# Four output products of a batch in the loop of the values' turn, output weights rounded a step later, in the first attention of a two-layer decoder kernel

## The reference

```python
def _L0_attn_ref(x, Wq, Wk, Wv, Wo):          # NH = 16, hd = 32
    q = (x @ Wq.T).reshape(B, T, NH, hd).transpose(0, 2, 1, 3)   # k and v alike
    att = einsum('bhtd,bhsd->bhts', q, k) / sqrt(hd) + causal mask
    w = softmax(att, axis=-1)
    z = einsum('bhts,bhsd->bhtd', w, v).transpose(0, 2, 1, 3).reshape(B, T, D)
    return z @ Wo.T
x = x + _L0_attn_ref(_layernorm(x), Wq, Wk, Wv, Wo)
```

## Time and profile before

| | us |
|---|---|
| median of 3 runs | 1908.64 (1906.13 to 1909.9) |
| the profiled execution | 1907.17 |
| its span, first to last instruction | 1905.7 |
| PE busy in the span | 1805.5 |
| DVE, ACT, POOL busy | 1113.3, 807.4, 1010.0 |
| mean granted PE clock | 0.986 |

### The profile page before, as it was taken

The page is one execution under the profiler, slowest core; times in us unless marked ns, Lnnn a source line. Parts: engine busy times, 40 slices in busy tenths (PEclk is TensorE's granted clock), DMA queues, the critical chain, the costliest instruction groups (busy, mean ns, idle before and its releaser), DMA issues. The chain is left out here.

```text
span 1905.7 us, 30804 instructions
## 1 busy us (share of the span) xinstructions
PE 1805.5 (95%) x10161; PEld 1565.8 (82%) x10167; DVE 1113.3 (58%) x2769; ACT 807.4 (42%) x2063; POOL 1010.0 (53%) x965
## 2 busy tenths in 40 slices
PE   7999989999999999999888999999999999999996
PEld 5888858788999999899667888888888888867795
DVE  6676785763333333335766666666666757566345
ACT  3767633222222222221256566666665433543231
POOL 3444341397883957895457456456453203116783
PEclk9999999999999999999999999999999999999998
DMA  3556430236653645554343234233331210012666
GB/s 116 173 155 205 144 138 0 78 145 226 231 199 126 214 144 180 191 153 127 90 112 95 68 92 117 57 89 93 84 78 56 74 50 1 24 50 84 213 214 195
DMA packets 104551, 232.54 MB, mean 122 GB/s; under 512 B 20672, under 2 KB 20928, under 8 KB 101328
## 3 DMA queue, kind: packets, MB, share of 16 engines
q1 hardware_dynamic: 84080, 144.31, 25.0%
q0 software_dynamic: 19744, 85.47, 13.6%
q10 hardware_dynamic: 576, 0.79, 0.2%
HBM read 126.23 MB, written 57.93 MB: 97 GB/s over the span
## 5 line engine op out<-in xcount | busy, mean ns | idle before, releaser
L712 POOL TENSOR_SCALAR a_E<-a_E,a_inv 128x128 f32<-128x128 f32 (+3 forms) x384 | 213.9, 575 | 237.7 <-DVE a_inv L848 237.7
L745 ACT ACTIVATE a_E<-a_E,a_top 128x512 f32<-128x512 f32 (+3 forms) x384 | 211.1, 565 | 6.0 <-DVE a_top L842 5.9
L153 PE MATMUL bank<-f_UH,f_XH 128*128 x596 | 200.5, 336 | 8.4 <-POOL f_UL L165 3.4
L153 PE MATMUL bank<-f_UL,f_XH 128*128 x596 | 193.2, 324 | 0.0
L153 PE MATMUL bank<-f_UH,f_XL 128*128 x596 | 193.2, 324 | 0.0
L842 DVE CUSTOM_DVE_ANT_0 a_E<-a_causal,bank 128x512 f32<-128x512 bf16 (+3 forms) x384 | 163.6, 480 | 43.0 <-PE bank L1023 31.5
L153 PE MATMUL bank<-a_PHL,a_VH 128*128 128x512 f32 (+3 forms) x768 | 181.1, 325 | 0.9 <-issue 0.6
L737 ACT ACTIVATE a_PHL<-bank 128x512 fp32r<-128x512 f32 (+1 forms) x288 | 131.0, 528 | 112.6 <-PE bank L1039 112.5
L1821 ACT ACTIVATE f_HH<-bank 128x256 fp32r<-128x256 f32 x220 | 59.8, 323 | 232.2 <-PE bank L2218 232.1
L165 DVE TENSOR_TENSOR a_PHL<-bank,a_PHL 128x512 fp32r<-128x512 f32 (+1 forms) x288 | 153.2, 585 | 5.1 <-ACT a_PHL L737 4.8
L1876 DVE TENSOR_TENSOR f_gate<-bank,f_gate 128x352 f32<-128x352 f32 x79 | 41.3, 522 | 192.1 <-PE bank L153 192.0
(11 more groups left out here) (407 smaller groups left out, 4864.8 us busy)
## 6 DMA issues: line engine op xcount, KB each, us to landing
f_uraw<-f_up POOLq DMA_DIRECT2D x18, 1408.0 KB, 6.7
f_xb<-table SPq DMA_DIRECT2D x86, 256.0 KB, 3.2
table<-f_ob SPq DMA_DIRECT2D x86, 256.0 KB, 2.7
table<-a_zeros SPq DMA_DIRECT2D x31, 512.0 KB, 4.3
f_draw<-f_down POOLq DMA_DIRECT2D x27, 512.0 KB, 4.5
a_g<-a_f SPq DMA_DIRECT2D x160, 64.0 KB, 2.0
a_raw<-a_qkv SPq DMA_DIRECT2D x36, 256.0 KB
f_uraw<-f_up POOLq DMA_DIRECT2D x9, 704.0 KB, 4.4
```

The lines of the kernel that those rows point to most:

```text
L153: m = pe.matmul(out, a, b, start=first and i == 0 and j == 0, stop=last and i == n - 1 and j == 2, skip_group_check=not check)
L712: e.tensor_scalar(self.E[sl][:, a], self.E[sl][:, a], self.inv[:, sl, i:i + 1], 0.0, ALU.mult, ALU.add).then_inc(*self.s_nrm.up(N, m - 1, i))
L745: x = e.activation(E, E, ACT.Exp, scale=-1.0, bias=self.top[:, sl, i:i + 1], accum_out=self.total[:, sl, i:i + 1])
```

## The change

The output products move. Before, a turn had at most two, beside the projections of keys and queries (n = 0, 1 for batch 0, and n = 4, 5 for batch 1). After, all four of a batch stand behind the T of a values' turn (n = 3 for batch 0, n = 7 for batch 1). The output weights of a step are rounded in turn 0 of the step after it (`SPLIT` 0: -1), not in turn 6 of the step itself, and the query weights are loaded two turns ahead of their rounding, not four. The rest of the diff brings branches under `self.beside`, which is False for both attentions, and helpers that give the same values as the terms that they replace: with `HALF = P`, `half(h)` is 0, `closes(h)` holds for the last head alone, and the three passes of the values' product are issued in the same order with the same flags. The loop runs two turns longer, because the last output products come in turns 35 and 39, not 36 and 37.

```diff
-            self.FILL = [[("P", K, 1), ("O", 0, -1), ("O", 1, -1)], [("P", 0, 1), ("O", 2, -1), ("O", 3, -1)],
-                         [("P", V, 1)], [("T", 1)], [("P", K, 0, 1), ("O", 4, -1), ("O", 5, -1)],
-                         [("P", 0, 0, 1), ("O", 6, -1), ("O", 7, -1)], [("P", V, 0, 1)], [("T", 0, 1)]]
-            self.SPLIT = {2: (K, 1), 3: (0, 1), 5: (V, 1), 6: (self.wt, 0)}
-            self.LEAD = {K: 3, 0: 4, V: 2, self.wt: 2}
+            self.FILL = [[("P", K, 1)], [("P", 0, 1)], [("P", V, 1)],
+                         [("T", 1)] + [("O", g, -1) for g in range(TT)],
+                         [("P", K, 0, 1)], [("P", 0, 0, 1)], [("P", V, 0, 1)],
+                         [("T", 0, 1)] + [("O", g, -1) for g in range(TT, NT)]]
+            self.SPLIT = {0: (self.wt, -1), 2: (K, 1), 3: (0, 1), 5: (V, 1)}
+            self.LEAD = {K: 3, 0: 2, V: 2, self.wt: 2}
...
-            if j + ahead < self.STEPS:
+            if 0 <= j + ahead < self.STEPS:
...
+                V, p = (b * TT + sblk), m % 2
+                passes = [(self.VH[:, h, V, :], self.PH[p][:, a]), (self.VH[:, h, V, :], self.PL[p][:, a])]
+                if not self.beside:
+                    passes.append((self.VL[:, h, V, :], self.PH[p][:, a]))
```

More of the change, by code:

```diff
@@ L544, in plan @@
         self.slot, self.free, self.fill_bank, self.score_bank = {}, {}, {}, {}
[L545 removed]
+        freed, turned, ring, self.staged = [[], []], [], 0, {}
         for m in self.loops:
@@ L563, in plan @@
                             continue
+                    if c == self.vt and self.beside:
+                        self.staged[j, b], self.free[x[1:]] = self.W[:, :], turned
+                        turned = [self.s_vt.after(N, j, b)]
+                        continue
                     s = self.slot[x[1:]] = len(self.slot) % 2
@@ L687, in pool @@
         e.memset(self.causal[:, :], 0.0).then_inc(*self.k.g.up())
-        for z in (self.VH, self.VL):
+        for z in (self.VH,) if self.beside else (self.VH, self.VL):
             e.memset(z[:, :, :, :].bitcast(F32), 0.0)
@@ L706, in pool @@
                     e.tensor_tensor(g, g, self.cos_sin[:, 1, :], ALU.mult).then_inc(*self.s_p2.up(N, *x))
+            if self.beside and 4 <= m < self.M + 4 and self.jobs[m - 4][3] == self.heads - 1:
+                j, b, r, h = self.jobs[m - 4]
+                e.wait_ge(*self.s_olo.after(N, j, r, b, self.half(h)))
+                e.tensor_tensor(self.QL[:, r, b * T:b * T + T], self.R[:, :], self.S[:, :], ALU.add).then_inc(
+                    *self.s_rest.up(N, j, r, b))
             if 1 <= m <= self.M:
@@ L761, in act @@
                 self._act_rotated(m - 1)
-            if 3 <= m < self.M + 3 and self.jobs[m - 3][3] == self.heads - 1:
+            if 3 <= m < self.M + 3 and self.closes(self.jobs[m - 3][3]):
                 j, b, r, h = self.jobs[m - 3]
+                own, bank = self.rows(h), self.k.bank[self.OB]
                 e.wait_ge(*self.s_av.after(N, m - 3))
-                e.activation(self.QH[:, r, b * T:b * T + T], self.k.bank[self.OB][:, :], ACT.Copy).then_inc(
-                    *self.s_ohi.up(N, j, r, b))
+                x = e.activation(self.QH[own, r, b * T:b * T + T], bank[own, :], ACT.Copy)
+                if self.beside:
+                    if m - 3 >= self.heads:
+                        e.wait_ge(*self.s_rest.after(N, *self.outputs_before(m - 3)))
+                    x = e.activation(self.S[own, :], bank[self.other_rows(h), :], ACT.Copy)
+                x.then_inc(*self.s_ohi.up(N, j, r, b, self.half(h)))
     def _act_rotated(self, m):
@@ L866, in dve, with _dve_low_values @@
                 self._dve_low_rotated(m - 1)
[L867 to L872, removed]
+            if not self.beside and 3 <= m < self.M + 3 and self.closes(self.jobs[m - 3][3]):
+                self._dve_low_values(m - 3)
+    def _dve_low_values(self, m):
+        e, N, (j, b, r, h) = self.k.dve, self.name, self.jobs[m]
+        own, a, key = self.rows(h), slice(b * T, b * T + T), (N, j, r, b, self.half(h))
+        e.wait_ge(*self.s_ohi.after(*key))
+        if self.beside and m >= self.heads:
+            e.wait_ge(*self.s_rest.after(N, *self.outputs_before(m)))
+        to = self.R[own, :] if self.beside else self.QL[own, r, a]
+        low_part(e, to, self.k.bank[self.OB][own, :], self.QH[own, r, a]).then_inc(*self.s_olo.up(*key))
     def _stats(self, loaded, tiles):
@@ L1049, in _pe_values @@
             e.wait_ge(*self.s_vlo.after(N, j, b))
-        if h == 0 and self.OB in emptied:
+        if self.opens(h) and self.OB in emptied:
             e.wait_ge(*emptied[self.OB])
@@ L1055, in _pe_values @@
                 a = slice(self.P_AT[sblk], self.P_AT[sblk] + T - sblk * P)
[L1056 to L1059, removed]
+                V, p = (b * TT + sblk), m % 2
+                passes = [(self.VH[:, h, V, :], self.PH[p][:, a]), (self.VH[:, h, V, :], self.PL[p][:, a])]
+                if not self.beside:
+                    passes.append((self.VL[:, h, V, :], self.PH[p][:, a]))
+                for x, (values, weights) in enumerate(passes):
+                    t = e.matmul(self.k.bank[self.OB][:, sblk * P:T], values, weights,
+                                 start=self.opens(h) and sblk == 0 and x == 0,
+                                 stop=self.closes(h) and ci == 2 and x == len(passes) - 1)
         t.then_inc(*self.s_av.up(N, m))
-        if h == self.heads - 1:
-            emptied[self.OB] = self.s_olo.after(N, j, r, b)
+        if self.closes(h):
+            emptied[self.OB] = self.s_olo.after(N, j, r, b, self.half(h))
     def projections_done(self):
```

44 lines of the change are left out of this document (38 added, 6 removed).

## The result

| | us |
|---|---|
| before, median of 6 runs | 1907.32 (1905.58 to 1909.9) |
| changed, median of 6 runs | 1919.98 (1918.07 to 1922.87) |
| changed to before | 1.0064, 95% interval 1.0051 to 1.0078 |
| the changed kernel's profiled execution, its span | 1920.84, 1919.4 |
| mean granted PE clock | 0.982 (before 0.986) |

The change makes the kernel 12.7 us slower. The forecast was 1922.5, in a range from 1914.5 to 1928.0, with 0.89 on slower.

A forecast was written before the change was run, and what follows sets the result against it. PE's pace was taken to bound the kernel. The terms -3.9 + 11.55 + 5.1 - 0.2 + 1.3 = +13.85 on 1907.17 gave 1921.0, or 1922.5 us against the median; range 1914.5 to 1928 us.

The forecast's parts named there:

- slower: Whole kernel: over 1912.4 us, chance 0.89; wait with two to four falls 0.55, none or one 0.2, five 0.1.
- 0.78 us behind each of five values' turns: Turns behind turns 11, 15, 19, 23, 27: projection starts unhindered, 0.78 us gained each, 3.9 us in all.
- fourth output product waits for the T's bank: Five values' turns: PE stands 2.31 us each until the T's bank is emptied, 11.55 us lost.
- granted clock falls: After PE's idle of about 2.15 us in values' turns: three of five fall, 1.7 us each, 5.1 us lost.
- end of the stage, beside the 0.78: Turns 28 to 30 gain 2.7 us, turn 31 to the last statistics loses 2.5; net -0.2 us.
- query weights' load in step 0: Step 0, turn 3: ACT stands 0 to 3.5 us for the late load, query moves start later; 1.3 us taken.
- output weights' load: Between rounding at n = 0 and use at n = 3: covered by the turns between, no cost.
- The Trainium skill's rule: PE's gaps in values' turns: too short for any clock fall, so the time would be the first rival's, 1917.4 us.
- The bank wait without the clock: Rival, values' turns: PE waits for the bank, no clock falls; +8.75, 1917.4 us; none or one fall, chance 0.2.
- Half the wait: Rival, steady turns: the bank is free a us earlier, no falls; +2.95, 1911.6 us; chance 0.06.
- faster: Rival: turns even out, nothing waits, if the T's bank is free by +4.13; -2.8, 1905.8 us; chance 0.05.
- the reading that PE bounds the stage: Turns 9 to 15: PE busy 51.39 of 52.00 us, no other engine over 36.01; PE's idle adds to the time.

The follow-up runs named there:

- changed_again: The changed kernel once more, without an edit; 1920.33 us, ratio 1.0075 to before.
- values_early: Changed kernel with, in values' turns, high parts ahead of exponentials and low parts ahead of the scores' low parts; query weights loaded four turns ahead; 1906.76 us.
- t_last: Changed kernel with the T behind the four output products in values' turns, not ahead of them; 1911.01 us, ratio 1.0028 to before.
- kept_busy: Changed kernel with the third output product of each values' turn issued four times, three thrown away; 1915.42 us, ratio 1.0047 to before.
- before_values_early: Kernel before, with the values' high and low parts taken early as in values_early, its own output product places and loads; 1904.35 us, ratio 0.9982.
- spread_order: spread_early with DVE's addition of the output product to X ahead of both low parts; 1905.03 us, ratio 0.9985 to before.
- before_load_late: Kernel before, with the query weights loaded two turns ahead, not four; 1909.48 us, ratio 1.0016 to before.
- spread: Changed kernel with output products one to a turn (two in turn 2, none in 0), ahead of the T; query weights four turns ahead; 1901.93 us.
- spread_early: spread with the values' high and low parts taken early as in values_early; 1913.54 us, ratio 1.0027 to before.

## Why the prediction was right

By its own steps, with what the traces show for each:

| step | predicted, us | shown |
|---|---|---|
| 0.78 us behind each of five values' turns | -3.9 | -3.9 |
| fourth output product waits for the T's bank | +11.55 | +11.7 |
| granted clock falls | 3 times, 1.7 each: +5.1 | 2 times, 3.0 in all; in changed_again 3 times, 4.5 in all |
| end of the stage, beside the 0.78 | -0.2 | -0.24 |
| query weights' load in step 0 | +1.3 | +1.05; in changed_again +2.5, with late moves of keys in it |
| output weights' load | 0 | +0.1; in changed_again +0.35 |
| sum | +13.85 | +11.7 with two falls, +13.2 with a third |
| the medians | +13.85 | +12.7; in changed_again +14.1 |

**What was luck.** The change's own terms add up to 11.7 us in the profiled execution, 2.1 less than forecast, because the clock's term was 2.1 too large. That its time, 1920.84, still lies on the forecast's 1921.0 is luck: 1.3 us of its difference to before arose ahead of turn 1 and 0.5 behind the stage, and neither is of the change. Luck is also in the number of falls, three of five from stretches of another kind; two and three came.

**The bank.** The fourth product was said to start at +6.44 of the turn, and it starts at 107.27 - 100.83 = +6.44. The turn was to take 9.13, and takes 9.16; over 4.10 + 2.72 that is 2.34 each. Only the idle time was too large, 2.15 against 1.91: the next matmul could have gone at 104.97 + 0.23, or +4.37, not +4.13, because the T and the nine matmuls take 0.24 us more than I counted with; the wait swallows that. values_early, t_last and kept_busy show from three sides that it is this bank: emptied earlier, the turn is 7.0; with another bank as the fifth, 7.87; with PE busy, still 9.16.

**The 0.78 us.** A turn with one projection takes 6.39 or 6.40. Before, a turn behind a values' turn took 8.53, less two output products of 1.36 in all 7.17; the difference is the 0.78. It is gone in the changed kernel, and the wait on POOL with it. before_values_early says more exactly what it was: 0.34 the T's bank, and 0.44 that goes with the length of the turn before.

**The clock.** The mechanism was right. PE's waiting or multiplying is the only difference between the changed kernel and kept_busy in those turns, and with the waits go the falls. The ratios put them at 3.2 to 5.3 us (0.0017 to 0.0028), the turns at 3.0 for two and 4.5 for three. The term that was off is the size of one: I took the missing part of the clock over a stretch, 1.7 us, and the turns are longer by 1.47 and 1.56 (1.41 to 1.57 in changed_again). The missing part of turn 15's stretch is again 0.15 x 11.5 = 1.7, so not all of it comes on the path. The number of falls isn't one number: two in two executions, three in a third. The Trainium skill's rule (page "TensorE: Matmul & The Clock Gate", section "HAM oscillation — how this bites in real kernels"), by which such gaps are too short to matter, doesn't hold here: waits of 1.91 us brought falls in seven of fifteen turns.

**The loads.** The term of step 0 was the estimate with the least under it (0 to 3.5, 1.3 taken) and came out at 1.05, about half from ACT's stand of 0.95 us and half from the query moves behind the load, which the prediction named without a price. A step that failed is the sentence that the output weights are covered by the turns between. Their use is three turns away, but ACT works in order and waits 2.12 us for them in turn 8, with the rest of its turn behind them. That cost PE 0.1 us in the changed kernel, where they reached ACT 3.49 us into turn 8 (84.29 - 80.80), and 1.7 to 2.0 us of turn 9 in values_early and spread_order, where it was 4.84 and 5.13.

**The rivals.** "The bank wait without the clock" was put at 1917.4; kept_busy, which is that case, gives 1915.4. "Half the wait" and "faster" needed the T's bank earlier; nothing freed it. The condition of "faster", low parts 2.3 us earlier, was met by values_early (104.07 against 106.33), and it gave 1906.76 where I had put 1905.8. Of the 1905.8, 1.3 is a late load that values_early doesn't have; against 1904.5 the difference is 2.3 us, and turn 9's 1.7 is the greater part of it. The chances of "slower" were not added up cleanly: its three cases make 0.85, and the other 0.04 would have to come from "half the wait", which lay at 1911.6, under the bound of 1912.4. And the earlier trace rows run on to 139 us, which is in turn 16, not 15; the reading that PE bounds the stage is the same.

What stays open: why the median of before_load_late is 2.9 us up when its trace shows 1.0, what held up the moves of the keys in changed_again, and what decides which of the values' turns fall.

## What to carry to other kernels

Count how many banks of a ring one turn takes, scores and fills together: where it takes a bank again, PE waits until the other engines have emptied it. Here the turn was 2.34 us longer for it; with the slow bank's taker moved to the end of the turn's it was 1.05, and with its emptying moved ahead in the other engines' order 0.19, and 0.19 more in the turn behind. Evening out short and long turns is worth at most what the short one costs its neighbour, 0.78 us here: one product beside the T got 0.58 of it (spread), four beside it with the bank emptied early 0.40. When an engine's order is changed, look at every bank that it frees in that turn, not only at the one that is meant: spread_early lost 8.5 us (1913.54 to 1905.03; 8.0 by the ratios) by one addition, 7.6 of it in waits and some 1.6 in a fall of the clock.

## What the runs showed of the hardware

- Idle gaps of PE of 1.91 us, in turns that leave it hardly any other idle time, brought the granted clock down in seven of fifteen turns, for about 1.5 us of lost time each. Gaps of 1.5 us did so once in five (spread_early); single ones of 1.5, 1.6 and 1.8 us in turn 9 of three executions didn't, and those of 1.2 us (five) and 0.8 us (five) never did.
- The fall comes after the wait, not with it: in turn 15 PE is at work again from 135.62, and its matmuls are slow only from 136.42 on.
- With the same instructions and the same gaps every second values' turn fell, in two executions 15 and 23, in another 11, 19 and 27. By that a forecast of such a kernel can't name the turns, and has to leave one fall, about 1.5 us, open.
- The issue of a load of weights at 50.39 reached ACT at 53.41, 3.0 us, where nothing large was ahead of it. Behind moves and clearings, the output weights issued at 79.94 reached it at 84.29, 4.35 us (5.2 in values_early). A clearing of the same 256 KB took 5.5.
